# An adaLN block with grouped attention: filler transposes in the first wait, another order of the first weights and waits, and a bias spread by a transfer

## The reference

```python
mod = (_silu(L0_c) @ L0_wmod).reshape(L0_c.shape[0], 6, 1, -1)
sa, ca, ga, sb, cb, gb = (mod[:, 0], mod[:, 1], mod[:, 2], mod[:, 3], mod[:, 4], mod[:, 5])
ga = (2 * (ga >= 0) - 1) * jnp.maximum(jnp.abs(ga), 0.25)
gb = (2 * (gb >= 0) - 1) * jnp.maximum(jnp.abs(gb), 0.25)
h = _layernorm(x, axis=-1) * (1 + ca) + sa
x = x + ga * _L0_attn_ref(h, L0_attn_wq, L0_attn_bq, L0_attn_wkv, L0_attn_bkv, L0_attn_wo)
h = _layernorm(x, axis=-1) * (1 + cb) + sb
x = x + gb * _L0_ffn_ref(h, L0_ffn_gate_w, L0_ffn_expert_w, L0_ffn_expert_b)
```

## Time and profile before

| | |
|---|---|
| median of 3 runs | 917.33 us |
| lowest and highest | 916.95 and 917.77 us |
| the profiled execution, its own time | 918.79 us |
| span in the profile | 917.1 us |
| PE, DVE, ACT, POOL busy | 871.5, 743.4, 541.5, 327.4 us |
| mean granted clock of PE | 0.984 |

### The profile page before, as it was taken

How to read it: one execution, slowest core, us unless ns; L and a number is a source line. 1 busy time by engine, 2 the same in 40 slices (tenths; PEclk the granted TensorE clock), 3 DMA queues, 4 the chain that set the end, 5 groups by cost and what they waited for, 6 DMA issues and landing times.

```text
span 917.1 us, 16962 instructions
## 1 busy us (share of the span) xinstructions
PE 871.5 (95%) x5399; PEld 774.1 (84%) x5399; DVE 743.4 (81%) x1685; ACT 541.5 (59%) x1249; POOL 327.4 (36%) x401
## 2 busy tenths in 40 slices
PE   5999999999999999999999999999999999897776
PEld 5788888888888888888888988888888888797574
DVE  6777888888888888877888888888889897785357
ACT  4577666666666666664766666666666665553152
POOL 4464122222222222231534444444322224864605
PEclk9999999999999999999999999999999999998778
DMA  7000710000000000300000000000000004423633
GB/s 241 7 12 13 240 49 13 12 11 11 11 11 11 11 12 18 104 6 1 24 1 13 13 13 13 12 13 13 13 13 12 13 13 144 143 83 116 186 119 116
DMA packets 36682, 43.09 MB, mean 47 GB/s; under 512 B 3092, under 2 KB 33846, under 8 KB 36534
## 3 DMA queue, kind: packets, MB, share of 16 engines
q1 hardware_dynamic: 34248, 35.94, 12.2%
q0 software_dynamic: 2304, 6.29, 2.1%
q10 hardware_dynamic: 64, 0.02, 0.0%
HBM read 32.02 MB, written 15.20 MB: 51 GB/s over the span
## 4 chain that ended last, share of the span: by engine, by line
PE 87%; DVE 5%; issue 2%; another core or an unknown queue 2%; ACT 2%; POOL 1%; DMA 1%; SPq 0%; POOLq 0%; ACTq 0%; DVEq 0%
PE ps_t L1080 13%; PE ps_s L969 8%; PE ps_s L973 8%; PE ps_s L970 8%; PE ps_o L961 7%; PE ps_o L965 7%; PE ps_o L962 7%; PE ps_m L969 3%; PE ps_m L973 3%; PE ps_m L970 3%; PE ps_m L961 3%; PE ps_m L965 3%; PE ps_m L962 3%; PE ps_o L1090 1%
## 5 line engine op out<-in xcount | busy, mean ns | idle before, releaser
L1437 ACT ACTIVATE pt_hi<-ps_t 128x512 fp32r<-128x512 f32 (+2 forms) x320 | 170.9, 534 | 128.3 <-PE ps_t L1080 122.2
L1487 ACT ACTIVATE probs<-ps_s,neg_max 128x128 f32<-128x128 f32 (+7 forms) x256 | 189.9, 742 | 79.5 <-DVE neg_max L1867 77.3
L1876 DVE TENSOR_TENSOR pt_lo<-ps_t,pt_hi 128x512 fp32r<-128x512 f32 (+2 forms) x320 | 192.5, 602 | 17.6 <-ACT pt_hi L1437 12.1
L1867 DVE TENSOR_REDUCE neg_max<-ps_s 128x1 f32<-128x128 f32 (+7 forms) x256 | 192.5, 752 | 3.7
L1080 PE MATMUL ps_t<-ident,probs 128*128 128x128 f32 x1152 | 188.6, 272 | 1.0 <-DVE pt_lo L1876 0.9
L722 POOL TENSOR_TENSOR q_lo<-raw,q_hi 128x512 fp32r<-128x512 f32 x60 | 77.3, 1289 | 313.0 <-ACT q_hi L1437 313.0
L1080 PEld LDWEIGHTS ps_t<-ident,probs 128*128 128x128 f32 x1152 | 141.9, 141 | 21.1 <-DVE pt_lo L1876 4.9
L969 PE MATMUL ps_s<-k_hi,q_hi 128*128 128x512 f32 (+2 forms) x354 | 148.6, 420 | 3.9 <-ACT probs L1487 3.9
L1914 DVE SCALAR_TENSOR_TENSOR acc<-ps_m,rsum,acc 128x256 f32<-128x256 f32 x256 | 111.4, 476 | 16.3 <-PE ps_m L973 15.6
L973 PE MATMUL ps_s<-k_hi,q_lo 128*128 128x512 f32 (+2 forms) x354 | 123.3, 348 | 0.0
L970 PE MATMUL ps_s<-k_lo,q_hi 128*128 128x512 f32 (+2 forms) x354 | 122.7, 347 | 0.0
(11 more groups left out here) (332 smaller groups left out, 1729.8 us busy)
## 6 DMA issues: line engine op xcount, KB each, us to landing
slot_out_dram<-y_slot SPq DMA_DIRECT2D x38, 128.0 KB, 1.8
wq_raw<-in_L_attn_wq_dram SPq DMA_DIRECT2D x32, 128.0 KB, 2.3
wo_raw<-in_L_attn_wo_dram SPq DMA_DIRECT2D x32, 128.0 KB
wkv_raw<-in_L_attn_wkv_dram SPq DMA_DIRECT2D x2, 1024.0 KB, 6.6
acc<-in_L_attn_x_dram SPq DMA_DIRECT2D x2, 1024.0 KB, 15.1
we_raw<-in_L_ffn_expert_w_dram SPq DMA_DIRECT2D x1, 2048.0 KB, 8.3
slot_rows<-slot_rows_dram SPq DMA_DIRECT2D x2, 1024.0 KB
slot_rows_dram<-in_L_attn_x_dram SPq DMA_DIRECT2D x1, 1920.0 KB, 17.2
```

What stands on the lines that cost most here:

```text
L1437: return nc.scalar.activation(dst, src, ACT.Copy, scale=scale)
L1487: nc.scalar.activation(probs[par][:, prob_offset(i):prob_offset(i) + w], ps_s[:, i % 2, col:col + w], ACT.Exp, bias=neg_max[:, par, i:i + ...
L1867: nc.vector.tensor_reduce(neg_max[:, par, i:i + 1], ps_s[:, i % 2, col:col + w], AXIS_X, ALU.max, negate=True).then_inc(max_set, 1)
L1876: nc.vector.tensor_tensor(pt_lo[:, q % PT, lo:CH], ps_t[:, q % 2, lo:CH], pt_hi[:, q % PT, lo:CH].bitcast(F32), ALU.subtract).then_inc(pt_ ...
```

## The change

Five edits. (1) PE makes 32 transposes of the identity into a bank that nobody reads, right after turning the rows of c. (2) ACT no longer makes both halves of `wk_hi` ahead of the first `hidden`, but one after each of the first two. (3) PE waits for only two steps of `modt_set` ahead of the first queries; the third is waited for ahead of the second half of them, which write the bank that `gate_columns` reads. (4) The product that spread the value bias over the partitions is gone, with its row of ones, its row load on ACT's queue, and DVE's copy. (5) In its place SP issues a transfer that writes the bias row to all 128 partitions, between two loads that were there.

```diff
+WARM_TURNS = 32
...
+            sp.dma_start(v_bias[:, :].rearrange("p (g d) -> p g d", d=D),
+                         bkv_v[1, :, :].unsqueeze(0).to_broadcast([P, G, D])).then_inc(vb_set, 16)
...
-            pool.memset(ones_row[:, :], 1.0).then_inc(const_set, 1)
...
-            pe.wait_ge(const_set, 4)
+            pe.wait_ge(const_set, 3)
...
+            for _ in range(WARM_TURNS):
+                pe.transpose(ps_o[:, 0:P], ident[:, :], ident[:, :])
...
-                        if u == 2:
-
-                            pe.matmul(ps_m[:, :], ones_row[0:1, :], vb_row[0:1, :], start=True,
-                                      stop=True).then_inc(vb_mm, 1)
                         if u == 4:
-                            pe.wait_ge(vb_set, 1)
                             modulate(1)
...
-                    pe.wait_ge(modt_set, 3)
+                    pe.wait_ge(modt_set, 2)
...
                     pe.wait_ge(o_lo_set, n0 * NC)
+                else:
+                    pe.wait_ge(modt_set, 3)
                 queries(n0, 0, b, 1, ps_o)
...
-            act.dma_start(vb_row[0:1, :].rearrange("o (g d) -> o g d", d=D), bkv_v[1:2, :, :]).then_inc(small_in, 16)
...
-            cut_weights(0, 0)
             act.wait_ge(modt_set, 1)
             for u in range(NC * KE):
                 hidden(0, u)
+                if u < KE:
+                    cut_weights(0, 0, (u,))
...
-                        if u == 3:
-                            dve.wait_ge(vb_mm, 1)
-                            nc.vector.tensor_copy(v_bias[:, :], ps_m[:, :]).then_inc(vb_set, 1)
...
-                    dve.wait_ge(vb_set, 1)
+                    dve.wait_ge(vb_set, 16)
```

More of the change, by code:

```diff
@@ L235, in adaln_block @@
         gate_rows = at("gate_rows", [EXPERTS, E], F32, v_at + 18432)
-        vb_row = at("vb_row", [1, CH], F32, v_at + 20480)
-        ones_row = at("ones_row", [1, P], F32, v_at + 22528)
         sig_tmp = at("sig_tmp", [P, 3, KE * B], F32, v_at + 23552)
@@ L445, in adaln_block @@
         sig_exp, silu_set = sem("sig_exp"), sem("silu_set")
-        modt_mm, modt_set, vb_mm, vb_set = sem("modt_mm"), sem("modt_set"), sem("vb_mm"), sem("vb_set")
+        modt_mm, modt_set, vb_set = sem("modt_mm"), sem("modt_set"), sem("vb_set")
         var_set, rstd_set, xn_set = sem("var_set"), sem("rstd_set"), sem("xn_set")
@@ L636, in _ @@
                       allow_small_or_imprecise_dtypes=True).then_inc(const_set, 1)
-            pool.wait_ge(const_set, 4)
+            pool.wait_ge(const_set, 3)
             def inverse_deviations(lo, hi, count):
@@ L1025, in _ @@
                 turn_normalised(u)
-            pe.wait_ge(small_in, 4 * 16)
+            pe.wait_ge(small_in, 3 * 16)
             pe.transpose(ps_o[:, 0:nb], bias_rows[:, :], ident[0:nb, 0:nb])
```

## The result

The changed kernel takes 913.30 us (median of 8 runs, 913.06 to 914.97) against 917.09 us for the kernel before in the same session (8 runs, 915.63 to 917.77). The ratio is 0.9962, 95% interval 0.9953 to 0.9972: 3.5 us faster by the ratio, 3.8 by the medians. Forecast were 914.5 us and a gain of 2.8 us. The profiled execution of the changed kernel took 913.07 us (span 911.3); that of before took 918.79, more than any of its 8 timed runs. So the 5.8 us between the two profiled spans overstate the change, and the stages have to be read one by one.

What follows compares the result with a forecast made beforehand. Bound: PE nearly everywhere, then DVE's chain from the first queries, so only time ahead of the first head counts. 0.97 + 1.45 + 0.65, about 3.0, less 0.2: gain 2.8, 917.33 to 914.5 us; range 913.2 to 918.3.

Steps and rivals of the forecast that it cites:

- The turns raise the clock: 32 identity transposes on PE before the first modulation: 2.4 GHz from 7.0 us, 4.2 us after they begin; done at 8.4.
- What the clock gives: First modulation product in 1.95 us, not 3.54; ACT starts 1.75 us earlier; keys begin at 16.25, against 17.22.
- The key weights between the planes: ACT's new order puts key weights between its first modulations: gives back 0.8 of the 1.75 us.
- The value bias: Without the bias product and its wait, 1.15 and 0.3 us leave PE's path among the keys; the transfer costs nothing.
- The first queries: PE no longer waits 1.5 us for the gate columns; DVE is the bound, so only 0.65 us are won.
- The finish line: DVE's start of the first head's `queries_raw`: from 38.72 to about 35.7 us, and earlier there means earlier at the end.
- The sum: Whole start stage: 0.97 + 1.45 + 0.65 = 3.07, in round numbers 3.0 us, less 0.2 for DVE's chain: gain 2.8.
- the turns do not raise the clock: Rival, before the first modulation: transposes stay at 1.2 GHz, loss of 0.4 or 1.2 us, 917.7 to 918.5; chance 0.28.
- they do not overlap: Rival, before the first modulation: each transpose takes its listed 0.42 or 0.27 us; 918.7 or 924 us; chance 0.05.
- the high clock holds to the keys: Rival, at the keys: nine slow products take half the time; finish near 34.9, gain 3.8, 913.5 us; chance 0.12.
- The transfer: Rival, bias load ahead of the second x: it holds up DVE, about 916.5 us; chance 0.03.

Runs made afterwards that it cites:

- old_act_order: Changed kernel with both halves of the high key weights again ahead of ACT's first modulation (edit 2 undone); 889.37 us, ratio 0.9952 to the kernel before.
- held_clock: Changed kernel with further identity transposes (8, 6 and 10) in PE's waits ahead of the keys; 888.26 us, ratio 0.9935 to the kernel before.
- same_before: The kernel before, run again with nothing changed for a second profile; 893.61 us, ratio 0.9997.
- turns_only: The kernel before with the 32 identity transposes alone (edit 1); 893.72 us, ratio 0.9999.
- bias_product: Changed kernel with the value bias again by product, copy and wait (edits 4 and 5 undone); 891.86 us, ratio 0.9981 to the kernel before.
- order_only: The kernel before with ACT's new order of the key weights alone (edit 2); 893.92 us, ratio 1.0005.
- same_after: The changed kernel, run again with nothing changed for a second profile; 889.43 us, ratio 0.9956 to the kernel before.
- held_old_order: Changed kernel with ACT's old order (edit 2 undone) and further transposes (26 and 2) in PE's waits; 888.66 us, ratio 0.9947 to the kernel before.

## Why the prediction came out, point by point

The time (914.5) and the range were right; the account behind it was right in parts, and that the total came out so near is partly luck, as two of its terms erred in opposite ways.

- **The turns raise the clock: right.** The modulation product took 1.84 to 1.92 us in every profile with turns, never 3.5. The moment was taken as 4.2 us after they begin; it was 2.7 and 6.0 in two profiles.
- **What the clock gives: right for ACT, wrong behind it.** ACT started at 11.42 and 10.74 (forecast 11.05), the keys at 16.62 and 16.11 (forecast 16.25). The step that failed is "I expect it at 1.2 GHz again when they begin, and as long as before (3.7 us)". The clock was at 1.2 GHz again, but for 5.3 us in the first profile, and on the mean of the seven profiles with the new order and unfilled waits 1.8 us longer than of the five with the old one, which at half speed is about 0.9 us (an estimate). This is the size of what the turns and the new order had won, and the runs agree: all edits 0.9956, edits 3 to 5 alone 0.9959, each within 0.0014. Filling PE's waits gave 1.1 us back beside old_act_order on the same chip, and 1.9 by the ratio to the changed kernel's (held_clock). So that the lost clock costs time is shown by that run, while how much of it falls to which wait rests on one profile for each kernel.
- **The key weights between the planes: its price is not settled.** It was taken as 0.8 us. Beside the turns it is nothing that can be told, without them 2.3 us, in the kernel before 0.4 with an interval past zero. The working missed its other side, that the old order lets POOL slow DVE's normalisation from 1.4 to 3.3 us.
- **The value bias: right mechanism, too small.** The term was 1.45 us; undoing it in the changed kernel cost 2.2 to 2.4. The transfer cost nothing on the path: DVE never waited for `v_bias` or for the second x.
- **The first queries: right by the rows.** 0.65 us was the term, 0.66 us the idle time in the row; the ratio (0.7 us) and the medians (1.3) agree, but cannot tell it from nothing.
- **The finish line.** It was put at 35.7, 3.0 us sooner. It came at 36.81 in the first pair, 1.9 sooner, and at 35.02 in the second, 5.3 sooner. What was won there did pass to the end, but one pair of profiles does not give its size.
- **The sum.** Edits 3 to 5 were put at 2.1 us and gave 3.7 (2.5 to 4.9 by the interval); edits 1 and 2 at 1.0, less 0.2, and gave nothing that can be told. The two errors cancelled, which is luck. Part of the excess may be the clock's fall in the middle of the keys, which two profiles of kernels with the old bias product show (same_before, turns_only) and three others with it do not (before, bias_product, order_only); no profile without that product has it. The mean clock of the timed runs of before fits it; that it is this fall in them is argued, not shown.
- **The rivals.** That the turns do not raise the clock, and that they do not overlap, both fell: the product behind them never took 3.5 us, and 32 of them took 5.1 to 6.6 us in all. That the high clock holds to the keys did not happen by itself; made to happen, its `queries_raw` was at 34.52 (forecast 34.9), and the gain 5.8 us by the ratio (forecast 3.8; the interval is 4.5 to 7.1). The transfer held up nobody.

## What to carry to other kernels

Filler work that raises PE's clock pays only if PE stays at work until the long products begin; otherwise the earlier start can be paid back in slower products. A wait well ahead of them is enough: here the clock fell 3 to 5 us before the keys in five of the seven profiles that left the waits open. Judge such an edit by the product spacing at the next dense stretch, and by several profiles, since the moment of the rise moved by over 3 us between two executions of one kernel. A small product with a copy and a wait between dense stretches can cost more than its length: look whether the clock falls behind it. And test edits one by one even when their sum comes out: here three of the five gave as much as all five.

## What the runs showed of the hardware

- 32 f32 transposes of an identity (128x128), and nothing else, raised PE from 1.2 to 2.4 GHz: the product behind them took 1.84 to 1.92 us in all nine profiles with turns (22 of them in one), and 3.54 or 3.55 in the five without.
- Raised in this way, the clock fell again at 12.2 us in same_after and at 13.4 in old_act_order, while PE waited 1.6 and 3.7 us for DVE. With these waits filled by further transposes it did not fall (held_clock, held_old_order).
- With 1 us of idle time and 16 modulation matmuls of 2 columns each behind it, the granted clock fell while PE was at work (rows of same_before); in turns_only the idle time was 0.39 us. With 0.15 us (before, bias_product) it did not fall.
- DVE's four normalisations of 128x256 took 1.38 us alone and 2.81 to 3.38 us beside POOL's subtraction (3.28 in the rows of turns_only).
- One program took 917 us beside the changed kernel at first, and 894 on each of the three chips of the experiments, though like PE instructions of its first 780 us lie within 1.7 us of each other in the two profiles. 22 of the 24 us between the profiles lie between 840 and 885 us. In the second one PE has no gap there (windows of same_before, then of the first profile of before; the columns are those of the windows above):

```profile
840.00:850.00 10.00, 10.00 (x49) 8.42 (x48) 6.04 (x25) 3.00 (x8) 7.56 (x9) 1.00 0.53 157
...
860.00:870.00 10.00, 10.00 (x80) 9.69 (x80) 7.25 (x19) 7.24 (x22) 3.10 (x4) 1.00 0.93 320
```

```profile
840.00:850.00 10.00, 5.66 (x27) 5.16 (x28) 3.05 (x24) 1.99 (x7) 4.24 (x5) 0.68 0.36 120
...
860.00:870.00 10.00, 4.45 (x25) 3.43 (x23) 1.84 (x5) 0.75 (x3) 7.56 (x9) 0.87 0.47 139
```

Why the end stage, which gathers and scatters rows through memory, is so much longer in the first profiles stays open: no run tests it. Between 840 and 880 us the granted clock fell twice in each of the two first profiles (at 843.5 and 867.4, and at 841.4 and 861.9), and in none of the twelve profiles of the experiments.
